# Residual tiles loaded beside the first sweeps, five samples summed in the last of them, bands loaded behind it, and attention's first tiles loaded early

## The reference

```
x1 = x + dyn_conv(norm(x))      # 3x3 convolution, kernel mixed from 4 experts per sample
s1 = sweeps(norm(x1))           # down, up, right, left: row = row + relu(conv1d_9(previous row) + b)
x2 = x1 + s1
x3 = x2 + attention(norm(x2))   # linear attention with rope, plus a 3x3 depthwise "lepe" convolution
out = x3 + sweeps'(norm(x3))    # four sweeps again, other weights
```

## Time and profile before

| what | us |
|---|---|
| median of 3 runs | 3129.11 |
| the profiled execution, its span | 3132.45, 3130.7 |
| last sweep L1 ends (last L212) | 1337.8 |
| first sum of the local part starts | 1344.87 |
| taps start, ScalarE's last keep ends | 1425.06, 1582.1 |
| first transpose of attention | 1599.66 |

### The profile page before, as it was taken

The page is one execution under the profiler, slowest core; times in us unless marked ns, Lnnn a source line. Parts: engine busy times, 40 slices in busy tenths (PEclk is TensorE's granted clock), DMA queues, the critical chain, the costliest instruction groups (busy, mean ns, idle before and its releaser), DMA issues. The chain is left out here.

```text
span 3130.7 us, 71818 instructions
## 1 busy us (share of the span) xinstructions
PE 2747.3 (88%) x25712; PEld 2482.8 (79%) x25712; DVE 2172.1 (69%) x5174; ACT 1363.0 (44%) x2113; POOL 288.4 (9%) x801
## 2 busy tenths in 40 slices
PE   5888879999999999917969998878999999999791
PEld 3666669999999999913447777758999999999791
DVE  7888846666666666687018888886666666666865
ACT  3766642246632222236436666643225662222120
POOL 1112110000000000045000101010000000000602
PEclk9899989999999999958979999998999999999795
DMA  4334230000000000087054877856000000000758
GB/s 89 81 90 99 67 124 0 0 0 0 0 0 0 0 0 0 0 233 198 1 87 73 120 104 102 116 73 107 0 0 0 0 0 0 0 0 0 121 94 127
DMA packets 735622, 164.89 MB, mean 53 GB/s; under 512 B 728209, under 2 KB 728849, under 8 KB 730641
## 3 DMA queue, kind: packets, MB, share of 16 engines
q1 hardware_dynamic: 608928, 136.86, 22.7%
q10 hardware_dynamic: 126576, 26.41, 5.4%
HBM read 96.13 MB, written 67.11 MB: 52 GB/s over the span
## 5 line engine op out<-in xcount | busy, mean ns | idle before, releaser
L269 PE MATMUL L_conv<-L_x_hi,L_w_hi 128*128 128x256 f32 x5040 | 1251.0, 283 | 46.5 <-DVE L_w_lo L236 28.7
L269 PE MATMUL L_conv<-L_x_hi,L_w_lo 128*128 128x256 f32 x5040 | 1249.5, 283 | 0.0
L156 ACT ACTIVATE L_row_b<-S,L_bias 128x256 f32 (+1 forms) x1008 | 514.2, 510 | 1168.9 <-DVE L_x_hi L210 1158.0
L269 PEld LDWEIGHTS L_conv<-L_x_hi,L_w_hi 128*128 128x128 f32 x5040 | 958.7, 190 | 49.5 <-issue 28.9
L269 PEld LDWEIGHTS L_conv<-L_x_hi,L_w_lo 128*128 128x128 f32 x5040 | 957.0, 190 | 0.0
L220 DVE SCALAR_TENSOR_TENSOR S<-L_conv,L_neg_bias,L_row_b 128x256 f32 x1008 | 487.7, 484 | 517.5 <-PE L_conv L273 516.7
L273 PE MATMUL L_conv<-L_x_lo,L_w_hi 128*128 128x256 f32 x5040 | 771.3, 284 | 4.9 <-DVE L_x_lo L212 4.8
L273 PEld LDWEIGHTS L_conv<-L_x_lo,L_w_hi 128*128 128x128 f32 x5040 | 677.7, 190 | 7.4 <-DVE L_x_lo L212 7.4
L212 DVE TENSOR_TENSOR L_x_lo<-S,L_x_hi 128x256 fp32r<-128x256 f32 x1016 | 455.3, 448 | 34.7
L210 DVE TENSOR_SCALAR L_x_hi<-S 128x256 fp32r (+1 forms) x1016 | 316.7, 312 | 35.3
L604 PE MATMUL dc_conv<-dc_xz_hi,dc_w_hi 128*128 128x512 f32 x384 | 171.3, 446 | 6.5 <-DVE dc_w_lo L731 6.5
(11 more groups left out here) (177 smaller groups left out, 2896.4 us busy)
## 6 DMA issues: line engine op xcount, KB each, us to landing
dc_raw<-x SPq DMA_DIRECT2D x32, 512.0 KB, 6.6
x_scratch<-dc_raw SPq DMA_DIRECT2D x16, 1024.0 KB, 7.4
lp_xr<-x_scratch SPq DMA_DIRECT2D x16, 1024.0 KB, 7.0
x_scratch<-lp_xr SPq DMA_DIRECT2D x32, 512.0 KB, 7.7
at_res<-x_scratch SPq DMA_DIRECT2D x32, 512.0 KB, 10.5
x_scratch<-at_res SPq DMA_DIRECT2D x64, 256.0 KB, 5.3
fs_buf<-x_scratch SPq DMA_DIRECT2D x32, 512.0 KB, 6.7
at_G<-x_scratch ACTq DMA_DIRECT2D x56, 256.0 KB, 5.8
```

Source lines behind the costliest of these rows:

```text
L156: nc.scalar.activation(row_b[p][:, :, :], line(k, at_step(k, i), p), ACT.Identity, bias=bias[:, k:k + 1]).then_inc(row_b_ready[p], 1)
L269: nc.tensor.matmul(out, w[:, k, s * P:(s + 1) * P], x_hi[p][:, s:s + J, :], start=(s == 0 and n == 0), stop=False)
```

## The change

Tensors of a new class `Shared` live from the L1 sweeps to the end of attention. Its five tiles are the residual ring; three of them are later G0, G1 and the rotations, one holds attention's small constants and the y tiles, one is a T tile. Then:

- SP loads the first five x1 tiles beside the L1 sweeps, in place of the bands.
- In sweep 3, GpSimd adds S to a quarter (16 columns, 128x512) of each of the five tiles, three times (quarters 3, 2, 1), each time when those columns are final. Six steps later VectorE puts one bn_stats of such a quarter between the two halves of each of five steps. In the local part the samples 0 to 4 need only quarter 0.
- The bands are loaded at the start of the local part by ScalarE's queue, between avg and the bias; TensorE waits for them in four groups of 16 columns.
- x2 in DRAM has the layout of the tiles ([B, 128, 2048]), is stored in one DMA a sample, and read by attention in halves (a residual tile in four DMAs instead of two).
- At the end of the local part SP waits for all normalisations and stores, loads the six constants and G of samples 0 and 1, and VectorE fills only the four outer columns of G.

The core of the diff:

```diff
+class Shared:
+    def add_quarter(self, eng, n, g):
+        part = slice(g * QUARTER, (g + 1) * QUARTER)
+        cells = self.xr[n][:, :, part]
+        return eng.tensor_tensor(cells, cells, columns_of(self.S, n)[:, :, part], ALU.add)
+    def early_sync(self, sp):
+        for n in range(RING):
+            self.load_residual(sp, n)
+    def early_pool(self, pool, new_ready, done_before):
+        for n in range(RING):
+            pool.wait_ge(self.x1_in[n], 16)
+        for g in (3, 2, 1):
+            for p in range(2):
+                pool.wait_ge(new_ready[p], done_before(3, STEPS - g * QUARTER))
+            for n in range(RING):
+                self.add_quarter(self.nc.gpsimd, n, g).then_inc(self.quarter_summed, 1)
+    def early_vector(self, dve, step):
+        at = 0
+        for g in (3, 2, 1):
+            ready = STEPS - g * QUARTER + RING + 1
+            several(at, ready)
+            for n in range(RING):
+                step(3, ready + n, 0)
+                dve.wait_ge(self.quarter_summed, (3 - g) * RING + n + 1)
+                self.quarter_stats(n, g).then_inc(self.early_stats, 1)
+                step(3, ready + n, 1)
+            at = ready + RING
+        several(at, STEPS)
...
# local_part, SP
             for n in range(B):
                 sp.wait_ge(x2_ready, n + 1)
-                for q in range(2):
-                    sp.dma_start(x2[n].rearrange("c (i q) w -> q c i w", q=2)[q],
-                                 xr[n % RING][q * HALF:(q + 1) * HALF, :, :]).then_inc(x2_stored[n % RING], 16)
+                sp.dma_start(x2[n], xr[n % RING].rearrange("p i w -> p (i w)")).then_inc(x2_stored[n % RING], 16)
...
+            sp.wait_ge(normed, B)
+            for u in range(RING):
+                sp.wait_ge(x2_stored[u], 16 * len(range(u, B, RING)))
+            shared.load_constants(sp, *constants)
+            sp.wait_ge(pads_ready, 4)
+            shared.load_normalised(sp, x2, 0, 0)
+            shared.load_normalised(sp, x2, 1, 1)
# local_part, ScalarE
             act.dma_start(avg[:, :], group_avg).then_inc(consts_in, 16)
+            bands.load(act)
             act.dma_start(lb[:, :], lepe_b...).then_inc(consts_in, 16)
# local_part, TensorE (the wait for consts_in, 2 * 16, ahead of the first group stays)
-            pe.wait_ge(bands.loaded, 8 * 16)
             pe.wait_ge(normed, NB)
             for w in range(W):
+                if w % 16 == 0:
+                    pe.wait_ge(bands.loaded[w // 16], 2 * 16)
# local_part, VectorE
             def front(n):
                 x, u = xr[n % RING], n % 2
+                if n < RING:
+                    dve.wait_ge(shared.early_stats, 3 * RING)
+                    shared.add_quarter(nc.vector, n, 0).then_inc(x2_ready, 1)
+                    dve.wait_ge(x2_ready, n + 1)
+                    return chain.mark(shared.quarter_stats(n, 0)), shared.bn[:, n, :, :]
# attention
-            sp.wait_ge(set_up, 6)
-            load_g(sp, 0, 0)
             load_res(0, 0)
-            load_g(sp, 1, 1)
...
-            for t in G:
-                nc.vector.memset(t[:, :, :], 1.0).then_inc(set_up, 1)
```

More of the change, by code:

```diff
@@ L249, in _ @@
                         split(p, line(2, 0, p), 2 * STEPS + 2)
-                with dve.Fori(0, STEPS) as i:
-                    for p in range(2):
-                        step(k, dve.snap(i), p)
+                if k == 3 and final:
+                    final.early_vector(dve, step)
+                else:
+                    with dve.Fori(0, STEPS) as i:
+                        for p in range(2):
+                            step(k, dve.snap(i), p)
         @block.tensor
@@ L845, with local_part @@
 GROUP_EVERY = 7
 NORM_LAG = 8
-def local_part(nc, ctx, S, bands, affine, x1, x2, group_avg, lepe_b):
+def local_part(nc, ctx, S, bands, affine, shared, x2, group_avg, lepe_b, constants):
     def sb(name, shape, dt=F32):
@@ L854, in local_part @@
     sem = semaphores(nc, ctx, "lp")
-    xr = [sb(f"xr{u}", [P, J, W]) for u in range(RING)]
+    xr, x1_in = shared.xr, shared.x1_in
     avg = sb("avg", [P, P])
@@ L1002, in _ @@
                 if n < B:
-                    mark = front(n)
+                    sums = front(n)
                 if n >= 2:
@@ L1008, in _, with attention @@
                 if n < B:
-                    middle(n, mark)
+                    middle(*sums)
+            dve.wait_ge(normed, B)
+            for u in range(RING):
+                dve.wait_ge(x2_stored[u], 16 * len(range(u, B, RING)))
+            for pad in shared.pads():
+                nc.vector.memset(pad, 1.0).then_inc(pads_ready, 1)
 HEADS, HD = 8, 8
 ROWS = 8
-def attention(nc, ctx, S, affine, x2, x3, consts, rotations, wq_in, wk_in, bq_in, bk_in):
+def attention(nc, ctx, S, affine, shared, x2, x3):
     def sb(name, shape, dt=F32):
@@ L1021, in attention @@
     sem = semaphores(nc, ctx, "at")
-    G = [sb(f"G{u}", [P, J // 2, 2 * W + 2]) for u in range(2)]
-    T = [sb(f"T{u}", [P, J // 2, P]) for u in range(2)]
+    G, rot, cst, wq, wk, b_raw, y = shared.G, shared.rot, shared.cst, shared.wq, shared.wk, shared.b_raw, shared.y
+    g_in, consts_in = shared.g_in, shared.consts_in
+    T = [sb("T0", [P, J // 2, P]), shared.turned]
     res = [sb(f"res{u}", [P, C, J]) for u in range(2)]
@@ L1701, in early_sync, with early_vector, early_pool @@
             self.load(sp, item)
-    def early_pool(self, pool, new_ready, count):
+    def early_vector(self, dve, step):
+        with dve.Fori(0, STEPS) as i:
+            for p in range(2):
+                step(3, dve.snap(i), p)
+    def early_pool(self, pool, new_ready, done_before):
         for p in range(2):
-            pool.wait_ge(new_ready[p], count)
+            pool.wait_ge(new_ready[p], done_before(3, STEPS - PART))
         for item in range(B):
```

174 lines of the change are left out of this document (102 added, 72 removed).

## The result

| | kernel before | changed kernel |
|---|---|---|
| median of 15 runs each, same chip (us) | 3131.0 | 3142.74 |
| lowest and highest | 3125.55, 3138.73 | 3132.9, 3153.31 |
| the profiled execution, its span | 3132.45, 3130.7 | 3146.61, 3144.8 |

The ratio is 1.0032, 95% interval 1.0020 to 1.0045: slower, by more than the 0.2% that can be told from no change, and above the upper end of the range.

The account below looks back on a forecast made before the run. Bounds by stage: TensorE in the sweeps, VectorE in the local part's first 85 us, DMA and two fills at attention's start. +9.9 - 1.2 - 13.1 = -4.4 from 3132.45 gave 3128.0 (median 3124.7), range 3104 to 3138.

Parts of the forecast that it names:

- part 3: Attention's start: G and constants loaded during the taps, first transpose earlier, -13.1 us; attention itself 0.
- Part 1: Fourth sweep: GpSimd's 15 additions in three bursts delay VectorE's turns, 3.3 us a burst, +9.9 us.
- The statistics: Fourth sweep: VectorE's 15 statistics fit in its free time between the halves of a step, 0 us.
- third rival: Fourth sweep: TensorE's clock falls in each GpSimd burst, 7.3 us a burst, 22 in all, total 3136.8; 20%.
- Part 2: Front of the local part: time saved on five samples' sums is mostly spent waiting for the lepe bias, -1.2 us.
- T: Local part's front: moment the lepe bias lands behind the bands, 23.8 us after 1339.75, at 1363.6.
- first rival: Local part's front: the bias is not held by the bands, -21.8 us there, total 3104; 16%.
- 20 us spent standing: Local part's front: VectorE's 20 us saved on sums go in standing at sample 0's variance until the bias lands.
- second rival: Attention's opening: TensorE keeps full clock, -6 us more, total 3119; 16%.
- the one term set at nothing: Attention itself: a residual tile by four DMAs instead of two, SP issuing 5.8 us a sample instead of 4.4, 0.

Follow-up runs that it names:

- e5: Changed kernel plus an unused 32 bytes a partition ahead of attention's own tensors, so residual tiles start at a multiple of 256: 3129.05 us, ratio 0.9997.
- e14: Kernel before with attention's other tiles moved by 32 B and the residual tiles kept at a multiple of 256: 3130.99 us, ratio 1.0000.
- e12: Kernel before with 128 unused bytes between G and T, residual tiles at a multiple of 128 but not 256: 3131.28 us, ratio 0.9998.
- e9: The kernel of e8 with the old layout of x2 in DRAM: 3116.19 us, ratio 0.9948.
- e8: The kernel of e7 with the 15 quarter sums of the fourth sweep on VectorE instead of GpSimd: 3100.75 us, ratio 0.9906.
- e7: The kernel of e5 with the lepe bias's DMA issued ahead of the bands: 3112.8 us, ratio 0.9938.
- e2: Kernel before with only the new layout of x2 (one store a sample, a residual tile by four DMAs): 3131.6 us, ratio 1.0001.
- e1: Changed kernel with the old layout of x2 (two stores a sample, a residual tile by two DMAs): 3130.98 us, ratio 1.0004.
- e11: Kernel before with 64 unused bytes between G and the rest, residual tiles at a multiple of 64 only: 3146.13 us, ratio 1.0034.
- e6: Kernel before with 32 unused bytes between G and T, residual tiles 32 past a multiple of 64: 3141.4 us, ratio 1.0033.
- e13: Kernel before with the residual tiles alone moved by 32 B, all others keeping their place against 256: 3147.33 us, ratio 1.0046.
- e3: Changed kernel with the lepe bias's DMA issued ahead of the eight band DMAs on ScalarE's queue: 3126.34 us, ratio 0.9986.
- e4: Changed kernel, new x2 layout kept, with a residual tile loaded by two DMAs contiguous on the SBUF side: 3136.77 us, ratio 1.0013.
- e10: Changed kernel with residual loads of samples 2 to 15 cut to one row of 32 (x3 not the reference's): 3125.17 us, ratio 0.9966.

## Why the prediction was wrong

**The step that failed** is the last sentence of part 3: "In attention itself a residual tile comes by four DMAs instead of two: SP issues about 5.8 us a sample instead of 4.4, of 27; 0." Attention's body cost 20.6 us, not 0. The term was argued from SP's issue time alone. That was itself too small: 4.4 is twice the median issue, the loads of a tile took 5.7 us of SP on average in the body before and 10.5 after (of a round of 29.8, not 27). But it was not the cost, for e5 has 9.4 and a body of 450.3. The change did more than split the loads: it moved the tiles. Each body below is that of one trace.

| bodies, us | old layout | new layout |
|---|---|---|
| residual tiles at a multiple of 128 | 446.9 (before), 447.0 (e14), 450.0 (e12), 450.5 (e9) | 448.1 (e8), 449.3 (e7), 450.3 (e2), 450.3 (e5) |
| not at one | 457.3 (e1), 458.5 (e11), 459.6 (e6), 461.5 (e13) | 465.7 (e3), 467.5 (after); 461.9 with two loads (e4) |

With aligned tiles the layout, four DMAs and all, costs nothing that these traces can tell from their spread. The place alone costs about 10 us in the old layout, and about 17 with the four loads of the new one. Neither was weighed: DMA's share of 0.68 in the body before shows how little room it had, and no row of before could show an unaligned tile, but the addresses could have been compared. Why the four loads make an unaligned tile dearer stays open. The DMA share does not say: it is 0.78 to 0.80 in the four unaligned kernels of the old layout and 0.75 in the two that lose most.

**How busier DMA engines made TensorE late.** Over the bodies of all kernels the issue waits are 7.0 to 9.5 us at a DMA share of 0.67 to 0.69 (the eight aligned ones), 13.3 to 21.2 at 0.75 to 0.80 (the seven unaligned ones that load whole tiles), and 5.5 at 0.50 (e10). Instructions come over DMA too, in a queue of their own, 16 KB a piece, with these pieces, MB and share in the changed kernel's body (before, the same three numbers):

```profile
q8 instruction: 64, 1.05, 1.0%
```

The traces show that TensorE's stops end with them. In the stop that ended at 2040.60 (it began at 2036.79) a piece started between 2037.60 and 2037.70; its share over that 0.1 us, times 16, gives 1.43 us for the piece:

```profile
q8 instruction: 1, 0.02, 89.2%
```

TensorE went on 1.5 us behind its end. It is so each time: all 12 such stops in the changed kernel's body, all 10 before and all 149 in the sixteen traces end 1.2 to 1.9 us behind the end of an instruction piece. The pieces themselves are hardly slower (1.20 us on average, 1.16 before); in the longest stops they start later, this one 0.8 us after TensorE had already stopped, where each of the ten before had started at least 0.7 us ahead of it. So TensorE waited for instructions. That the busier engines held the pieces' start back fits the rows and was not tried by itself. The 10.3 us of longer matmuls fit the stretches at half clock behind such stops.

**Part 1, +9.9:** +10.3 measured, the clusters where they were expected. The first and the last L220 of the fourth sweep, before and then after:

```profile
1114.53 0.48 DVE L220 SCALAR_TENSOR_TENSOR S<-L_conv,L_neg_bias,L_row_b 128x256 f32 x1 [0.57 <-PE L_conv L273]
1336.55 0.48 DVE L220 SCALAR_TENSOR_TENSOR S<-L_conv,L_neg_bias,L_row_b 128x256 f32 x1 [0.46 <-PE L_conv L273]
```

```profile
1112.40 0.48 DVE L220 SCALAR_TENSOR_TENSOR S<-L_conv,L_neg_bias,L_row_b 128x256 f32 x1 [0.57 <-PE L_conv L276]
1344.67 0.48 DVE L220 SCALAR_TENSOR_TENSOR S<-L_conv,L_neg_bias,L_row_b 128x256 f32 x1 [0.59 <-PE L_conv L276]
```

One burst in the changed kernel's timeline of VectorE:

```profile
1163.86 0.48 DVE L220 SCALAR_TENSOR_TENSOR S<-L_conv,L_neg_bias,L_row_b 128x256 f32 x1 [0.46 <-PE L_conv L276]
...
1164.70 1.65 DVE L212 TENSOR_TENSOR L_x_lo<-S,L_x_hi 128x256 fp32r<-128x256 f32 x1
1166.28 0.47 DVE L220 SCALAR_TENSOR_TENSOR S<-L_conv,L_neg_bias,L_row_b 128x256 f32 x1
1166.79 1.11 DVE L210 TENSOR_SCALAR L_x_hi<-S 128x256 fp32r x1
...
1169.50 0.47 DVE L220 SCALAR_TENSOR_TENSOR S<-L_conv,L_neg_bias,L_row_b 128x256 f32 x1
```

Turns stand 2.4, 3.2 and 3.2 us apart in place of 1.77, with operations stretched as in the earlier trace rows. Turn by turn against the kernel before, the sweep falls behind by 3.1, 3.1 and 3.2 us in the three bursts, where 3.3 each was forecast. The statistics cost nothing that can be told, as forecast (e8). The third rival, a clock that falls in the bursts, did not come: 1.00 in the windows above.

**Part 2, -1.2:** -1.1 measured. TensorE waited 27.5 us for the bias, which was issued at 1352.2 and landed 19.6 us later, at 1371.8. Counted from the first band's issue at 1347.54 T came at 24.3 us (forecast 23.8), and the taps stood at T+60.4 (forecast 60.3). TensorE's waits there:

```profile
PE lp_group L1025 <- DVE lp_few L1075: 45.6, 8, 7.4
PE lp_group L1025 <- DMA lp_lb<-L_conv_lepe_b: 27.5, 1, 27.5
PE lp_taps L1032 <- ACT S L998: 9.5, 1, 9.5
```

The first rival falls with it: e3 moved the bias ahead, and VectorE's 20.9 us were 2.7. By the rule of the Trainium skill that the prediction cites (DMA: Bandwidth & Descriptors, Queues, rings and completion order) each engine consumes the descriptors of a queue in ring order, so a small transfer takes its turn behind what was queued before it, and here it did. But the prediction stopped short of its own finding: it named 20 us spent standing and did not ask what one line's order was worth. It was worth 17 (e3).

**Part 3, -13.1** (-12.4 to the first transpose, -0.7 behind it): -13.8 measured. The first transpose came 6.0 us behind the last tap's start instead of 19.1 (-13.1), and the opening took 31.4 us at clock 0.66 against 32.1 before (-0.7). The second rival, an opening at full clock, did not come.

The sum of these three parts was right to a microsecond (-4.6 against -4.4; the taps between them, forecast at 0, took 0.9 more). The range missed because the one term set at nothing had no bound above it.

## What to carry to other kernels

When a change adds tiles to SBUF, compare the start of every tile that DMA fills in small pieces, before and after: off a multiple of 128 B the pieces of 128 B took 25% more DMA time on average here, and a few spare bytes mend it. Put an edit's small constants ahead of its big loads on a queue, and keep elementwise work off GpSimd in a stretch where VectorE has gaps of its own. And undo one part alone only beside its counterpart, doing it alone: e1 by itself put the blame on the layout, which was the part worth keeping (e9).

## What the runs showed of the hardware that was not expected

- Tiles loaded and stored in DMA pieces of 128 B: 18.1 ns of an engine's time a piece where the tile starts 32 B past a multiple of 128, 14.4 at a multiple (e13, e14). The loads pay and the stores hardly (14.6 in e10), and in the changed kernel only two of a tile's four loads (12.9 ns a piece in one, 28.4 in the next).
- TensorE, with no operand late, stopped for up to 3.8 us inside an unrolled loop, and each of 149 such stops ended 1.2 to 1.9 us behind the landing of a 16 KB instruction piece. They grew from 9.5 to 21.2 us over the body, and its clock fell behind the longest.
- GpSimd's additions of 128x512 took 1.6 us each beside VectorE, 24 us in 15, and cost 10.3 us of the sweep; the same 15 on VectorE took 1.05 each and cost nothing measurable.
